# The last sequence of an attention and mixture-of-experts kernel: the sequence ahead is routed two chunks sooner, and the last sixteen scatters keep at most two in flight

## What is computed

```python
x = x + _layernorm(_L0_attn_ref(_layernorm(x), Wq, Wk, Wv, Wo, ...))   # gated linear attention, 16 heads
# then a mixture of experts, 8 experts, 2 for each token
logits = jnp.einsum('bth,eh->bte', x, router_w) + router_b
topv, topi = jax.lax.top_k(logits, TOP_K)
gates = jax.nn.softmax(topv, axis=-1)
# for each expert e, with w = sum(gates * (topi == e)):
h = jax.nn.silu(x @ gate_w[e].T) * (x @ up_w[e].T)
acc = acc + (h @ down_w[e].T) * w
x = x + _layernorm(acc)
```

## Time and profile before

| | |
|---|---|
| Median of 3 runs | 1258.31 us (1257.32 to 1260.11) |
| Profiled execution: its time, and its span | 1258.35 us, 1256.5 us |
| Stage 1 | 0 to about 829 us of the span |
| The last sequence's chunks | about 766 to 800 us |
| PE, DVE, ACT, POOL busy | 92%, 61%, 51%, 44% of the span |

### The profile page before, as it was taken

How to read it: one execution, slowest core, us unless ns; L and a number is a source line. 1 busy time by engine, 2 the same in 40 slices (tenths; PEclk the granted TensorE clock), 3 DMA queues, 4 the chain that set the end, 5 groups by cost and what they waited for, 6 DMA issues and landing times.

```text
span 1256.5 us, 29203 instructions
## 1 busy us (share of the span) xinstructions
PE 1160.0 (92%) x8910; PEld 944.3 (75%) x8910; DVE 769.1 (61%) x2380; ACT 640.3 (51%) x1653; POOL 556.3 (44%) x686
## 2 busy tenths in 40 slices
PE   8999999999999999999999999659999999999895
PEld 4867768768668678677687686559999989998762
DVE  5667777787777777777767776623333333333327
ACT  3646647547446556565475474324444444444336
POOL 2244563554554654645636544323333333333326
PEclk9999999999999999999999999779999999999998
DMA  7001010110110110100101101325111111111434
GB/s 275 10 27 28 15 42 8 34 34 17 34 34 10 40 32 10 42 18 24 42 8 34 34 4 35 134 71 148 47 48 50 48 45 50 48 45 47 157 126 193
DMA packets 59676, 67.50 MB, mean 54 GB/s; under 512 B 6896, under 2 KB 49664, under 8 KB 59264
## 3 DMA queue, kind: packets, MB, share of 16 engines
q1 hardware_dynamic: 48720, 41.10, 10.4%
q0 software_dynamic: 8448, 17.45, 4.2%
q10 hardware_dynamic: 2480, 8.61, 2.2%
HBM read 37.98 MB, written 29.15 MB: 53 GB/s over the span
## 4 chain that ended last, share of the span: by engine, by line
PE 68%; DVE 15%; issue 8%; ACT 4%; DMA 3%; DVEq 1%; POOL 1%; another core or an unknown queue 0%; POOLq 0%; ACTq 0%; SPq 0%
PE pO L761 9%; PE pO L594 9%; PE pO L599 7%; PE pA L578 6%; PE pW L627 5%; PE pA L752 4%; PE pA L753 4%; PE pJ L752 4%; PE pJ L753 4%; PE pT L610 3%; DVE S_raw L1127 2%; DVE qT L1113 2%; PE pJ L627 2%; PE pJ L512 2%; DVE ss L1157 2%
## 5 line engine op out<-in xcount | busy, mean ns | idle before, releaser
L1621 POOL DMA_INDIRECT expert_out<-y,tail x136 | 130.6, 960 | 261.3 <-ACT y L1020 234.1
L871 ACT ACTIVATE sq<-pO 128x512 f32<-128x512 f32 x128 | 75.9, 593 | 214.8 <-PE pO L594 161.0
L594 PE MATMUL pO<-vJ,aT 128*128 128x128 f32 x1024 | 145.4, 286 | 14.3 <-DVE aT L1150 14.3
L594 PEld LDWEIGHTS pO<-vJ,aT 128*128 128x128 f32 x1024 | 129.4, 197 | 37.2 <-issue 34.3
L1539 POOL DMA_INDIRECT expert_rows<-x1n,rowi x120 | 120.6, 1005 | 55.5 <-issue 35.9
L1157 DVE TENSOR_REDUCE ss<-sq 128x8 f32<-128x512 f32 x128 | 87.1, 681 | 83.4 <-ACT sq L871 81.9
L761 PE MATMUL pO<-wdown_sb,vJ 128*128 128x128 f32 x1088 | 132.7, 275 | 0.0
L761 PEld LDWEIGHTS pO<-wdown_sb,vJ 128*128 128x128 f32 x1088 | 126.8, 192 | 0.0
L1405 DVE TENSOR_TENSOR vJ<-pA,kJ 128x256 f32<-128x256 f32 x136 | 57.5, 425 | 104.4 <-ACT kJ L1009 104.4
L599 PE MATMUL pO<-S_mid,qT 128*128 128x128 f32 x896 | 118.3, 275 | 0.0
L599 PEld LDWEIGHTS pO<-S_mid,qT 128*128 128x128 f32 x896 | 109.1, 192 | 0.0
(11 more groups left out here) (234 smaller groups left out, 2373.5 us busy)
## 6 DMA issues: line engine op xcount, KB each, us to landing
xt<-expert_rows SPq DMA_DIRECT2D x69, 130.0 KB
xa<-x SPq DMA_DIRECT2D x16, 256.0 KB, 2.8
xr<-x SPq DMA_DIRECT2D x16, 256.0 KB
after_attention<-x SPq DMA_DIRECT2D x16, 256.0 KB
arena<-after_attention ACTq DMA_DIRECT2D x8, 512.0 KB
expert_rows<-zeros SPq DMA_DIRECT2D x8, 390.0 KB
expert_out<-y,tail POOLq DMA_INDIRECT x136
wgate_sb<-wgate SPq DMA_DIRECT2D x1, 2048.0 KB, 9.9
```

The lines of the kernel that those rows point to most:

```text
L594: last = mm(o[:, g, h, :, :], aT[:, c % 2, h, g * P:(g + 1) * P], vJ[:, c, h, :], start=(h == 0 and g == 0), stop=(c == 0), skip_group_che ...
L1621: g.indirect_dma_start(out=ys_dram, in_=y[:, k, :], in_offset=None, out_offset=bass.IndirectOffsetOnAxis(ap=tail[:, k, 1:2].bitcast(U32), ...
```

## The change

In the last sequence alone (`more` false), the steps that route sequence 14 move ahead: PE's `logits` from chunk 4 to 3 and `ranks` from 5 to 4; ACT's `router_T` from 3 to 2 and `router_exp` from 5 to 4; DVE's `choose` from 4 to 3, and `places`, `end_i`, `weigh` and `next_goals` from 6 to 4. POOL's scatters of sequence 14 all stand behind `ready_to_scatter` in one loop. Each of the last sixteen scatters raises one of two new semaphores, `late[0]` or `late[1]` by copy, and waits before it issues until the one before it on the same semaphore has landed. SP waits for both. The first fourteen sequences are the same as before.

```diff
--- before.py
+++ after.py
@@ -339,6 +339,7 @@
         g2_ready = sem("g2_ready")
         kept = sem("kept")
         scattered = sem("scattered")
+        late = [sem(f"late{n}") for n in range(2)]
         dve_step = sem("dve_step")
         counts_ready = sem("counts_ready")
         ends_ready = sem("ends_ready")
@@ -440,7 +441,9 @@
 
             sp.wait_ge(counts_ready, 1)
             ends = [sp.value_load(cum_i[0:1, e:e + 1], min_val=e + 1, max_val=TILES) for e in range(E)]
-            sp.wait_ge(scattered, 16 * 2 * NT * S)
+            sp.wait_ge(scattered, 16 * 2 * NT * (S - 2))
+            for k in range(2):
+                sp.wait_ge(late[k], 16 * 2 * NT)
 
             def load_rows(first):
                 sp.dma_start(xt[:], xs_dram[bass.ds(first, ROWS)].rearrange("(t p) h -> p t h", p=P))\
@@ -645,9 +648,9 @@
                         gate_logits(i + 1, c - 2)
                     if routed and c == 2:
                         router_transposes(i - 1, i - 1, x1n)
-                    if routed and c == 4:
+                    if routed and c == (4 if more else 3):
                         logits(i - 1)
-                    if routed and c == 5:
+                    if routed and c == (5 if more else 4):
                         ranks(i - 1)
 
             def router_transposes(i, n, rows, tiles=WHOLE):
@@ -915,14 +918,14 @@
                     if more and c == 2:
                         gates(i + 1, 0)
                         gate_logs(i + 1, 0)
-                    if routed and c == 3:
+                    if routed and c == (3 if more else 2):
                         router_T(i - 1)
                     if more and c == 3:
                         gates(i + 1, 1)
                     if more and c == 4:
                         gate_log(i + 1, 1)
                         decays(i + 1, 0)
-                    if routed and c == 5:
+                    if routed and c == (5 if more else 4):
                         router_exp(i - 1)
                     if c == 7:
                         merged_rstd(i, 2)
@@ -1196,19 +1199,19 @@
                         router_stats(i - 1)
                     if more and c in (3, 5):
                         gate_scan(i + 1, (c - 3) // 2)
-                    if routed and c == 4:
+                    if routed and c == (4 if more else 3):
                         choose(i - 1, i - 1)
-                    if routed and c == 6:
-                        if more:
-                            weigh(i - 1, x1n[:])
-                            next_goals(i - 1)
+                    if routed and more and c == 6:
+                        weigh(i - 1, x1n[:])
+                        next_goals(i - 1)
                         places(i - 1, rowi)
-                        if not more:
-
-                            dve.wait_ge(base_ready, FIRST + i)
-                            v.tensor_copy(end_i[:], base[:]).then_inc(ends_ready, 1)
-                            weigh(i - 1, x1n[:])
-                            next_goals(i - 1)
+                    if routed and not more and c == 4:
+                        places(i - 1, rowi)
+
+                        dve.wait_ge(base_ready, FIRST + i)
+                        v.tensor_copy(end_i[:], base[:]).then_inc(ends_ready, 1)
+                        weigh(i - 1, x1n[:])
+                        next_goals(i - 1)
                     if c in (3, 5, 7):
                         merged_stats(i, (c - 3) // 2)
                     if more and c == 7:
@@ -1535,10 +1538,10 @@
                 pool.wait_ge(rowi_ready, i + 1)
                 settle(pool)
 
-            def scatter(t, k):
+            def scatter(t, k, landed=scattered):
                 g.indirect_dma_start(out=xs_dram, in_=x1n[:, k, t, :], in_offset=None,
                                      out_offset=bass.IndirectOffsetOnAxis(ap=rowi[:, k, t:t + 1], axis=0))\
-                    .then_inc(scattered, 16)
+                    .then_inc(landed, 16)
 
             def scatter_last(n, tiles):
                 pool.wait_ge(tail_ready, (S - 1 + n) * 2 + 2)
@@ -1549,9 +1552,11 @@
                 settle(pool)
                 for t in tiles:
                     for k in range(2):
+                        pool.wait_ge(late[k], (NT + t) * 16)
+                        settle(pool)
                         g.indirect_dma_start(out=xs_dram, in_=last_rows[:, k, t, :], in_offset=None,
                                              out_offset=bass.IndirectOffsetOnAxis(ap=last_rowi[:, k, t:t + 1], axis=0))\
-                            .then_inc(scattered, 16)
+                            .then_inc(late[k], 16)
 
             def scattered_all(i):
 
@@ -1585,11 +1590,12 @@
                     residual(i, 1)
                 if routed:
                     ready_to_scatter(i - 1)
+                if routed and more:
                     for n in range(2):
                         scatter(0, n)
                 if more:
                     residual(i, 2)
-                if routed:
+                if routed and more:
                     for n in range(2):
                         scatter(1, n)
 
@@ -1604,9 +1610,12 @@
             with pool.Fori(2, S - 1) as i:
                 turn_and_mids(i)
             turn(S - 1, True, False)
-            for t in range(2, NT):
-                for n in range(2):
-                    scatter(t, n)
+            for t in range(NT):
+                for k in range(2):
+                    if t > 0:
+                        pool.wait_ge(late[k], t * 16)
+                        settle(pool)
+                    scatter(t, k, late[k])
             pool.wait_ge(pad_out, 16 * (E + 1))
             for n, tiles in enumerate(HALVES):
                 scatter_last(n, tiles)
```

## The result

| | before | after |
|---|---|---|
| Median, six runs each on one chip | 1259.97 us (1257.32 to 1261.49) | 1253.42 us (1251.32 to 1257.05) |
| Ratio, with its 95% interval | | 0.9954 [0.9938, 0.9970] |
| Profiled execution: time, span | 1258.35, 1256.5 us | 1251.32, 1249.5 us |
| PE's first expert transpose | 828.88 | 819.84 |

The account below looks back on a forecast made before the run. The last scatter's issue (823.71 us), set by DVE, bounds the kernel: 1.85 and 3.12 us gained, 0.69 lost, so issue at 819.4, 4.28 sooner, and 1258.35 becomes 1254.1 us; range 1251.8 to 1258.4.

Parts of the forecast that it names:

- The block: DVE's twelve `places` and `weigh` instructions leave chunk 6 for chunk 4: 1.85 us off the path.
- The cover named: DVE's 1.34 us idle before chunk 6's first step absorbs the moved routing work, so the move costs nothing there.
- Rival 3: Chunks 3 to 5 have no room, so the routing's move gives nothing: 1255.9 us, chance 0.09.
- The gate: Waits between the last sixteen scatters: 3.22 us per pair instead of 2.53, adding 0.69 us in H1's four.
- The estimate of 2.15 us for a landing: Skill-based time for a 66 KB scatter to land, under a pair's 2.53 us; sum 0.7 us lower; not adopted.
- the rest of POOL's path: From sequence 14's second scatter at 796.0, seven steps of 3.22 us to a last issue at 818.5, 0.9 before DVE's.
- Rival 2: POOL's paced scatters become the bound, five steps at 5.2 us: slower, 1263.1 us, chance 0.11.
- The hole: Gap of 6.21 us behind sequence 14's first scatter, claimed to recur every 128 indirect DMAs and so kept.
- The stall: DVE's `places` of H1 takes 3.85 us against 0.73 for H0; the extra 3.12 us taken as gone.
- Rival 1: The extra time in `places` of H1 remains, gain only 1.16 us: 1257.2 us, chance 0.31.
- the merge: PE's last head merge, 2.05 us at full clock and 3.76 at half: up to 1.71 us possible gain, range only.
- The clock: PE's half-clock dip, range only: merge gain up to 1.71 us; experts' start between 2.14 lost and 2.7 won.

Follow-up runs that it names:

- c: The changed kernel once more, beside the kernel before on the same chip; 1254.34 us, ratio 0.9978.
- a: The changed kernel without the waits between the last sixteen scatters, so only the routing's move; 1252.55 us, ratio 0.9971 to the kernel before.
- h: The routing's move without the waits between scatters, measured again in another set; 1252.10 us, ratio 0.9960 to the kernel before.
- d: The changed kernel plus blank PE products, 20 behind the ranks of H0 and 50 behind those of H1; 1253.20 us, ratio 0.9985 to before.
- b: The kernel before plus the waits on all last sixteen scatters, routing not moved; 1260.40 us, ratio 1.0036.
- f: The changed kernel plus eight early extra scatters that write sequence 0's rows again to the same places; 1271.61 us (one run).
- e: The routing's move without waits between scatters, sequence 14's scatters held until the last sequence's second residual to form one unbroken run; 1253.19 us (one run).
- j: The kernel before with only the semaphores of the last sixteen scatters changed to two new ones, no waits between; 1259.24 us, ratio 1.0000.
- i: The kernel before, unchanged, profiled again; 1254.21 us (one run).
- k: The routing's move without waits between scatters, all scatters on the common semaphore of the kernel before; 1253.94 us, ratio 0.9947 to before.
- l: The routing's move without waits between scatters, plus blank PE products in three places (20, 52, 14); 1257.46 us, ratio 0.9987 to before.

## Why the prediction was right, and where it was right for a wrong reason

**The size.** 1254.1 us were forecast and 1253.42 measured. There is luck in this closeness: the forecast took 4.28 us from the 1258.35 of one profiled run, the median of the kernel before came out at 1259.97 with six runs, and so the gain is 6.55 between the medians (5.8 by the ratio). c gave 0.9978, a smaller gain on another chip. The gain is 0.2% to 0.5%, and "faster by over 0.2%" is what the six runs say.

**The block, 1.85 us.** Right to the hundredth, in every kernel that moves the routing: the residual starts at +20.95 where it was at +22.80. The cover named, the 1.34 us of idle time of the earlier trace rows, shrank by 0.75 and held. Rival 3 fell. Kernels a and h show that the routing's move carries the whole change; the block is 1.85 of its 5.1 us on the path (+55.36 to +50.25), and nearly all of the rest is the stall.

**The gate, +0.69 us.** Right as a price of H1's four where the changed kernel ran: 0.58 in after and 0.65 in c, a pair taking 3.10 us (810.38 to 813.48); it was 1.04 in d and 1.18 in b and f. The rows show 2.27 and 2.30 us for a landing and then 0.83 us until POOL starts again (3.10 less 2.27). The estimate of 2.15 us for a landing, worked out from the Trainium skill's page "DMA: Bandwidth & Descriptors", section "Anatomy of one DMA", would have made the gate free. The measurement decides: the gate isn't free. What the sum missed is the rest of POOL's path. It put 3.22 us on each of seven steps, and the two steps under the pads took 5.08 and 4.40. That only just stayed hidden in after, and in c it did not. Against kernel e the gate cost 0.9 and 1.7 us in all. Rival 2 named the right mechanism, for two steps and not for five: POOL's queue decides by 1.2 us in c, and fully in b, where it makes the kernel slower than before.

**The hole, 6.21 us, which "goes with the count".** This step failed. The hole was 3.20, and kernel f shows that the count does not set it. The trace of the kernel before could have told as much: it has the hole not once more in stage 2 but twice, and the one of 4.66 us, behind the 226th indirect DMA, fits no distance of 128. (It comes 113 behind the first, in the kernels with the common semaphore alone; kernel f has the new ones, so a count of that kind was not tested.) Two errors on POOL's path, a hole 3 us too large and two pairs 3 us too short, cancelled, which is why DVE still was the later one in after, as forecast.

**The stall, 3.12 us, taken as gone.** It was gone, and the reason given was wrong. The prediction called the extra time waits for DVE's own results, but the longest of the three, 1.58 us, is put down to "remote" in the earlier trace rows. It tied the stall to eleven scatters back to back; kernel e sends as many before the same instructions and has no stall. Kernel b has no stall with the routing unmoved. Kernel j has it elsewhere. Rival 1 (the stall stays) and the forecast both tied it to a place in the program or to its scatters, and neither fits the five traces that have it (before, i, j, k, l). What removes it from after and c is not shown. That is the largest term of the sum, and it was won with a wrong argument. Where a delay of 3.3 us is back, as in k, the routing's move is worth 3.6 us on the path (+50.19 to +46.59), with the merge's 1.71 among them; k's ratio is the best of all the same. A part of that is in the traces: a's last issue comes 1.73 us before k's, but its first result is scattered at +61.46 and k's at +61.85, since the clock came back sooner in k. The rest the profile of one execution doesn't explain.

**The clock, left out of the sum.** It gave 1.71 us at the merge in the profiled execution, the whole of the upper bound that the text had named. It isn't a sure gain: with the routing unmoved the merge was slow in all four profiles (before, i, b, j); with it moved it was fast in six of ten. At the other end neither bound was met: the experts began 5.2 us before the clock rose (819.84 to 825.0), where it had been 5.3. In this pair the clock came back as long after the work began as before, and the first result's scatter follows PE's first transpose by 10.39 us, where it was 10.45. That is not fixed: the clock rose between 4.3 us (i) and 7.5 us (f) behind PE's first transpose in the kernels without fillers, and the first result took 9.96 to 11.48 us. So an issue that comes 1 us sooner need not be 1 us off the end.

## What to carry to other kernels

A gate that bounds the transfers in flight is only free while its engine has time in hand: here it cost 0.9 to 1.7 us with the scatters sent early and made the kernel 0.36% slower without. Work taken off the one path that ends a stage is worth its rows exactly, if the place it goes to has an idle gap at least as long. A stall seen in one trace is a term of the sum only when a second trace of another build has it at the same place; ask for that before building a reason on it. And compare two profiles from an instruction that stands ahead of the change: here 3.0 of the 7.0 us between them had been won before the change acted.

## What was unexpected in the hardware

**Short drops of the clock.** Stage 1 runs the same code in all kernels but f, and yet POOL's normalisation started between 768.6 us (d) and 773.5 us (before). The two profiles differ in their clock there (0.98 and 0.99): seven short stretches at half clock in before, five in after, at other places. The runs of one kernel spread accordingly, 1247.5 to 1254.7 us in h. One profile against one profile can't show 0.2%.

**A delay that moves.** 3 to 5.5 us near the end of stage 1, on DVE or ACT, the longest waits released by an event that the profile calls remote. It changes its place with a semaphore's name, and shows in four of the eleven different kernels (before, j, k, l). Unexplained.

**A hole between two indirect DMAs** of 3.2 to 6.2 us behind the first scatter of sequence 14, and of 4.1 us at the 57th tile of stage 2 (1138.33 to 1142.38 in after). A third, of 4.66 us at the 50th tile, is in the three traces whose last scatters raise the common semaphore. They don't go with the count; the first is shorter and the third gone when the last scatters raise semaphores of their own. Unexplained.

**The price of a full queue on PE.** Eight tile counts that stood behind 85 products cost 2.8 us after the data was there. In the changed kernel, where PE idles, the eight loads take 5.4 us from the first start to the last end (811.14 to 816.50).
